# The layer norm of the next sequence's tokens, placed behind the fifth pair of heads instead of the first

## The reference, cut to what matters

```python
x = x + attn(_layernorm(x), Wq, Wk, Wv, Wo)      # 16 heads, sim = 50*tanh(sim/50), causal softmax
x = x + ffn(_layernorm(x), gate_w, gate_b, sw1, sb1, sw2, sb2, w1, b1, w2, b2)

def _layernorm(x, axis=-1, eps=1e-05):
    m = jnp.mean(x, axis=axis, keepdims=True)
    v = jnp.var(x, axis=axis, keepdims=True)
    return (x - m) / jnp.sqrt(v + eps)
```

## Time and profile before

| | |
|---|---|
| median of three runs | 2223.99 us (2222.87 to 2224.55) |
| the profiled execution's own time | 2222.78 us |
| its span, first to last instruction | 2221.1 us |
| mean granted clock of TensorE | 0.958 |
| busy share of PE, DVE, ACT, POOL | 88%, 67%, 64%, 45% |

### The profile page before, as it was taken

One profiled execution on the slowest core, in us unless ns is written; L12 is line 12 of the kernel. 1 busy time (PEld: TensorE's weight loads), 2 busy tenths in 40 slices (PEclk: granted clock), 3 DMA queues, 4 the chain that ended last, 5 costly groups with the idle time before them and its releaser, 6 DMA issues.

```text
span 2221.1 us, 39929 instructions
## 1 busy us (share of the span) xinstructions
PE 1953.5 (88%) x14653; PEld 1525.6 (69%) x14653; DVE 1495.0 (67%) x2803; ACT 1419.2 (64%) x2170; POOL 1003.5 (45%) x1195
## 2 busy tenths in 40 slices
PE   6889898989898989898989989898989876699898
PEld 4666676766666767676666767576767654699898
DVE  5467767676767686767676767676767685566565
ACT  6768575767676766767685857676767651344444
POOL 3434545453535353535353536353535442444344
PEclk9999999999999999999999999999999987799999
DMA  3000101010101010101010101010100012665564
GB/s 123 1 10 12 38 10 39 10 39 10 39 10 39 11 39 11 39 11 39 11 39 10 39 10 39 10 39 11 39 11 30 11 39 98 211 186 173 164 183 142
DMA packets 73665, 112.51 MB, mean 51 GB/s; under 512 B 9715, under 2 KB 52218, under 8 KB 73476
## 3 DMA queue, kind: packets, MB, share of 16 engines
q1 hardware_dynamic: 58468, 67.86, 10.5%
q0 software_dynamic: 15008, 42.10, 5.1%
HBM read 63.10 MB, written 48.65 MB: 50 GB/s over the span
## 4 chain that ended last, share of the span: by engine, by line
PE 43%; DVE 28%; ACT 21%; issue 7%; DMA 1%; POOL 0%; another core or an unknown queue 0%; POOLq 0%; DVEq 0%; SPq 0%; ACTq 0%
PE ring L1188 6%; ACT prob L590 5%; ACT prob L584 5%; PE bank_o L1230 5%; DVE norm L795 4%; DVE q_lo L784 4%; PE ring L1209 3%; DVE kT L779 3%; PE ring L1195 3%; PE ring L1214 3%; ACT kT L597 2%; ACT qT L607 2%; ACT qT L601 2%; DVE oTl L809 2%; PE ring L1136 2%
## 5 line engine op out<-in xcount | busy, mean ns | idle before, releaser
L508 POOL TENSOR_SCALAR_AFFINE_SELECT prob<-prob 128x256 f32<-128x256 f32 x512 | 219.2, 443 | 683.1 <-ACT prob L590 683.0
L584 ACT ACTIVATE prob<-ring 128x1024 f32<-128x1024 f32 (+1 forms) x384 | 328.1, 877 | 269.2 <-PE ring L1214 265.1
L779 DVE TENSOR_TENSOR kT<-ring,kT 64x512 fp32r<-64x512 f32 x256 | 176.3, 688 | 414.6 <-ACT kT L597 336.6
L1230 PE MATMUL bank_o<-prob,v 128*32 128x512 f32 (+3 forms) x4096 | 327.4, 463 | 103.3 <-DVE weighed L800 85.0
L520 POOL TENSOR_TENSOR key_sum<-prob 128x768 f32<-128x768 f32 x128 | 236.5, 1848 | 261.8 <-PE bank_d L1244 252.1
L590 ACT ACTIVATE prob<-prob 128x1024 f32<-128x1024 f32 (+1 forms) x384 | 344.0, 914 | 5.2
L1230 PEld LDWEIGHTS bank_o<-prob,v 128*32 128x32 f32 x4096 | 122.0, 115 | 284.3 <-issue 188.3
L1209 PE MATMUL ring<-qT,kT 128*128 128x256 f32 (+3 forms) x1024 | 244.2, 341 | 79.5 <-ACT qT L607 23.5
L1209 PEld LDWEIGHTS ring<-qT,kT 128*128 128x128 f32 x1024 | 168.9, 192 | 156.7 <-DVE q_lo L784 37.0
L795 DVE RECIPROCAL norm<-bank_d 128x512 f32<-128x512 f32 x64 | 214.7, 3355 | 26.5 <-PE bank_d L1244 25.5
L1214 PE MATMUL ring<-q_lo,kT 128*128 128x256 f32 (+3 forms) x1024 | 229.0, 325 | 0.0
(11 more groups left out here) (224 smaller groups left out, 4665.0 us busy)
## 6 DMA issues: line engine op xcount, KB each, us to landing
xin<-first SPq DMA_DIRECT2D x71, 257.0 KB
xin<-second SPq DMA_DIRECT2D x71, 129.0 KB
xin<-base SPq DMA_DIRECT2D x71, 128.0 KB, 2.1
x_next<-in_x SPq DMA_DIRECT2D x16, 512.0 KB, 4.6
x_res<-in_x SPq DMA_DIRECT2D x16, 512.0 KB, 3.8
raw_e<-in_w SPq DMA_DIRECT2D x4, 1024.0 KB, 6.8
first<-pad SPq DMA_DIRECT2D x9, 257.0 KB, 8.7
second<-pad SPq DMA_DIRECT2D x9, 129.0 KB, 8.1
```

The lines of the kernel that those rows point to most:

```text
L508: last = nc.gpsimd.affine_select(out=diag, in_=diag, compare_op=ALU.is_ge, fill=0.0, base=0, pattern=[[0, 2], [1, P]], channel_multiplier=-1)
L584: nc.scalar.activation(probs[p % PROBS][u][:, :, :], slot[:, :, 0:UNIT_COLS[u]], ACT.Tanh, scale=SCALE / SOFTCLAMP).then_inc(act_emptied, 1)
L779: last = nc.vector.tensor_tensor(kT[head_rows[1 - h], h, :], slot[r, 1, :], kT[r, h, :].bitcast(F32), ALU.subtract)
L1230: last = pe.matmul(bank_o[h * QD:(h + 1) * QD, j * P:N], v[:, j, f:f + QD], probs[(2 * quad + h // 2) % PROBS][u][:, h % 2, at:at + N - j ...
```

## The change

The block of five lines that does the layer norm of sequence i + 1 moves in DVE's loop from behind the work of p = 0 to behind `empty_gate(i - 1)` at p = 4. Nothing is added or removed; no other engine's program changes.

```diff
-                    if p == 0 and i + 1 < NSEQ:
-                        dve.wait_ge(xnext_loaded, 16 * (i + 2))
-                        layernorm_stats(1, x_next)
-                        layernorm_guess(1, i + 1)
-                        layernorm_newton(1, i + 1)
-                        layernorm_apply(1, i + 1, x_next, x_next, xn_ready)
                     if p == 1 and i >= 1:
                         weigh_values(i - 1, PAIRS - 1)
                         split_values(i - 1, PAIRS - 1)
...
                         if p == 7:
                             add_shared(i - 1)
+                    if p == 4 and i + 1 < NSEQ:
+                        dve.wait_ge(xnext_loaded, 16 * (i + 2))
+                        layernorm_stats(1, x_next)
+                        layernorm_guess(1, i + 1)
+                        layernorm_newton(1, i + 1)
+                        layernorm_apply(1, i + 1, x_next, x_next, xn_ready)
                     if p == 6 and i + 1 < NSEQ:
                         empty_turned1(i + 1)
```

## The result

The changed kernel takes 2238.93 us (median of six runs, 2234.43 to 2242.71) against 2224.27 us (six runs, 2222.87 to 2226.94): a ratio of 1.0064, 95% interval 1.0051 to 1.0077. It is slower by 0.64%, 14.7 us. The profiled execution took 2237.29 us, with a span of 2235.5 us, 14.4 us more than before.

A forecast was written before the change was run, and what follows sets the result against it. No engine alone bounds the kernel: the path changes engines, and PE waits on DVE. 2222.8 + 16.2 (fourteen sequences) + 1.5 (sequence 0) = 2240.5, plus 1.2 for the median: 2241.7, given as 2241 us; range 2220 to 2257.

The forecast's parts named there:

- the stall moves to the ring slot of the logits: Main forecast, 61%: at p = 5 PE's scores wait for DVE's late `empty_logits`, slightly dearer than the old wait.
- What is removed: At p = 1, PE's wait for `weighed`, 5.92 us, plus mean clock loss, 1.82 us: 7.74 us in each of 14 sequences.
- The shift at p = 5: `empty_logits` starts 6.7 us later behind a layer norm of 7.36 us; bounds 5.0 and 7.4 us.
- from there on it meets the additions as before: From `var_eps` on, the moved layer norm meets POOL's additions as at the old place; length 8.07 - 0.71 = 7.36 us.
- The clock's loss there: PE's lowered clock behind the new wait at p = 5 costs 2.2 us; bounds 1.4 and 3.0 us.
- Net per sequence: 8.9 us added at p = 5 less 7.74 removed at p = 1: +1.16 us, times 14 = +16.2 us.
- Sequence 0: Wait and clock removed at p = 1, `values` waiting 5.4 us at p = 5: between 0 and +4.7, taken as +1.5 us.
- The layer norm did not escape POOL: Rival, 10%: the layer norm passes POOL's additions unhindered at its new place, taking 5.64 us; 2206 to 2218 us.
- The clock does not drop: Rival, 5%: at p = 5 the clock stays up or its loss is hidden; only the 6.7 us stall counts; 2209 us.
- The even exchange: Rival, 14%: clock loss at p = 5 at its low end, 1.4 us, layer norm some tenths shorter; 2224 to 2228 us.
- the four: The rivals: short layer norm (10%), no clock drop or hidden loss (5%), even exchange (14%), old length and worst clock (10%).
- the seam: Between POOL's first two additions of p = 4: DVE goes first; the other order would change the stall by about 0.1 us.

The follow-up runs named there:

- e1: Changed kernel with the next sequence's layer norm at the end of p = 1 (sequence 0: before the last weight split), where DVE idled; 2109.57 us.
- e7: Kernel before, with PE computing the queries of p = 2 four more times ahead of its wait for `weighed`, sequences 1 to 14; 2197.25 us.
- e3: Changed kernel with PE computing unit 2 of the scores of p = 5 twelve more times in sequences 1 to 14; 2208.83 us.
- e5: Changed kernel, but in sequence 0 the layer norm stays at p = 0; 2232.97 us, ratio 1.0033 to the kernel before.
- e4: Changed kernel with POOL's three key additions of p = 4 waiting until the layer norm is done, sequences 1 to 14; 2222.68 us.
- e2: Changed kernel, but at p = 5 DVE empties the logits first, then does the layer norm, ahead of the reciprocal; sequence 0 keeps p = 4; 2186.29 us.
- e6: Changed kernel with the nine Newton instructions of the next sequence's layer norm left out; 2217.04 us, ratio 0.9961 to the kernel before.

## Why the prediction was right, point by point

The forecast was 2241 us against 2238.93 measured, slower by the mechanism named: the stall moves to the ring slot of the logits. But two of its terms were off in opposite directions, so part of the closeness is luck: the fourteen sequences were put 5.7 us too long, sequence 0 3.0 us too short. (The sum's last line, 2241.7, would round to 2242.)

- **What is removed**, 7.74 us a sequence: the distances show 7.72, e1 some 7.6, and e7 shows 1.7 of the clock's 1.8 us in it. Sequence 15 had been the right row to read it from.
- **The shift at p = 5**, 6.7 us: measured 8.10 - 1.77 = 6.33. The term that was too large is the layer norm's length, and the step behind it is "from there on it meets the additions as before". `rstd`, which starts a little later within POOL's addition than at the old place, is held 1.18 instead of 1.27 us, one small instruction fewer meets a mask, and the logits' first instruction follows 1.30 us behind the start of the last four, where the reciprocal followed after 1.40. 7.36 us of layer norm were 6.98.
- **The clock's loss there**, 2.2 us, taken as the middle of 1.4 and 3.0: 2.23 on average. That it is wholly on the path is shown by e3.
- **Net per sequence**, +1.16: measured +0.75, so 14 x 0.41 = 5.7 us too much.
- **Sequence 0**, +1.5 (0 to 4.7): measured +4.5 at its end, 3.0 us too little. I had taken the old length of the layer norm there without asking which POOL work arrives when nothing holds ACT back (e5).
- **The rivals.** The layer norm did not escape POOL; e4 shows what that would have been worth, 1.6 us a sequence of waiting, of which 0.4 went back to the clock. "The clock does not drop" is refuted by the 14 stretches, and that its loss is hidden by e3. The even exchange came closest of the four, and would have needed a clock loss of 1.4 us.
- **The pages' rules.** At the seam between POOL's first two additions DVE went ahead: `var_eps` started at 881.46, while the first addition ran until 881.55, and took its usual 0.17 us. POOL's second addition began 0.08 us behind the first's end, as at every seam between these two, so nothing shows it held. Held by DVE is POOL in sequence 0 of the changed kernel, where its first addition begins beside a DVE instruction that started 0.09 us earlier and takes 2.31 instead of some 1.83 us:

```profile
88.81 0.69 DVE L809 TENSOR_TENSOR oTl<-weighed,oTh 128x512 fp32r<-128x512 f32 x1
```

```profile
88.90 2.31 POOL L520 TENSOR_TENSOR key_sum<-prob 128x768 f32<-128x768 f32 x1 [3.70 <-PE bank_d L1244]
```

Both orders of the lock that the Trainium skill describes ("SBUF — State Buffer", "Who interferes with whom") are in the trace, then; at the new place the seam was worth no more than 0.1 us, as put. With the warning of "TensorE: Matmul & The Clock Gate" ("Why this matters for your kernels") in the Trainium skill against idle gaps above some 3 us the runs agree in the main: the clock fell behind all waits of 4.4, 4.6, 5.9 and 6.2 us and behind 13 of 14 of 3.3 us, and stayed full behind those of 0.3 and 0.4 us in e3 and e7. Near 3 us they show no sharp limit: in sequence 0 of the kernel before, the clock reads 1.00 behind a wait of 2.63 us and 0.50 behind one of 2.69 us.

## What to carry to other kernels

The same work on a helper engine cost 0, 4.6, 7.7 or 8.4 us a sequence at four places (e1, e2, the kernel before, the changed kernel), depending on the first thing queued behind it that another engine waits for: look for the place where that engine idles for long enough (here 9 us at the start of p = 2), rather than for a place further from the last stall, and let short instructions that free a buffer go first. A step of the same kernel in which the work is missing (here the last sequence) prices its removal better than the wait alone does. Count the lowered clock behind each long wait of the matrix engine as part of the wait's price; where the wait can't be removed, matmuls that only repeat a result can be worth their place.

## What the runs showed of the hardware that had not been expected

The loss behind a wait is no constant, and shortening the wait can raise it. With waits of 6.2, 4.6 and 4.4 us (the changed kernel, e4, e6) the loss was 2.23, 2.66 and 2.82 us. The traces show how: in these three the clock falls within the wait and is still low when PE goes on, and the loss is the part of that low stretch in which PE works. In sequence 7 it came back about 4 us behind the end of the 6.2 us wait of the changed kernel, and 5.3 us behind the end of the 4.6 us wait of e4 (stretches of the two):

```profile
887.10:891.00 3.90, 3.90 (x13) 3.51 (x13) 3.86 (x2) 1.02 (x1) 0.00 (x0) 0.50 0.00 0
891.10:897.00 5.90, 5.90 (x33) 5.08 (x33) 2.75 (x5) 5.58 (x9) 3.47 (x4) 1.00 0.01 3
```

```profile
881.50:886.70 5.20, 5.20 (x18) 4.81 (x19) 3.86 (x2) 2.13 (x3) 3.90 (x4) 0.50 0.02 3
886.80:893.00 6.20, 6.20 (x31) 4.95 (x30) 4.06 (x6) 5.55 (x10) 4.48 (x5) 1.00 0.00 0
```

From the second of the fourteen on, the sequences of e4 and e6 lay 112.6 us apart, as the calmest sequences of the kernel before did, though their waits differ. With PE kept busy they took the same time as well, 111.7 us in e3 and 111.4 in e7, while in the changed kernel they swung between 113.1 and 114.8 us, and the longest are those with the largest loss (sequence 8: clock 0.50, 114.8 us; sequence 10: 0.74, 113.2 us). So the swing comes from the clock. That it also pulls different kernels to the same distance is what the rows suggest; no run was made to show how.
